# First loads of x and context by batch, and transposes of the identity in TensorE's waits

## What is computed

```
x = x + tanh(g_xattn[l]) * xattn(layernorm(x), ctx)     # 32 query heads, 8 key/value heads of 128
x = x + tanh(g_ffn[l])   * ffn(layernorm(x))
# xattn: q = h @ Wq.T; k, v = ctx @ Wk.T, ctx @ Wv.T; q, k = rmsnorm(q), rmsnorm(k)
#        softmax(q k^T / sqrt(128) + mask) @ v, then @ Wo.T
```

## Time and profile before

| | |
|---|---|
| median of 3 runs | 1437.88 us |
| the profiled execution | 1436.61 us, its span 1434.8 us |
| TensorE (matmul) busy | 1364.0 us, 95% |
| VectorE, ScalarE, GpSimd busy | 959.0, 846.6, 629.4 us |
| mean granted TensorE clock | 0.982 |
| chain that ended last | TensorE 69%, issue 12%, VectorE 8%, GpSimd 6% |

### The profile page before, as it was taken

How to read it: one execution, slowest core, us unless ns; L and a number is a source line. 1 busy time by engine, 2 the same in 40 slices (tenths; PEclk the granted TensorE clock), 3 DMA queues, 4 the chain that set the end, 5 groups by cost and what they waited for, 6 DMA issues and landing times.

```text
span 1434.8 us, 26304 instructions
## 1 busy us (share of the span) xinstructions
PE 1364.0 (95%) x7915; PEld 1143.1 (80%) x7924; DVE 959.0 (67%) x1971; ACT 846.6 (59%) x3270; POOL 629.4 (44%) x667
## 2 busy tenths in 40 slices
PE   5999999999999999987878899999999999999897
PEld 4888888888888888864645688888888888888786
DVE  4678787887878786477777655555555555557565
ACT  4656666666666666655455566566656666665341
POOL 2437666565656575443333334333333334341132
PEclk9899999999999999998989999999999999999999
DMA  7011210211111111001000110101010100100001
GB/s 272 1 51 47 64 51 18 78 36 55 51 62 51 57 51 57 31 1 45 1 29 1 35 48 30 45 29 44 29 44 29 44 29 23 50 0 1 0 16 45
DMA packets 33688, 59.23 MB, mean 41 GB/s; under 512 B 2784, under 2 KB 25952, under 8 KB 29536
## 3 DMA queue, kind: packets, MB, share of 16 engines
q1 hardware_dynamic: 33632, 58.54, 12.3%
HBM read 56.43 MB, written 2.10 MB: 41 GB/s over the span
## 4 chain that ended last, share of the span: by engine, by line
PE 69%; issue 12%; DVE 8%; POOL 6%; ACT 3%; DMA 1%; SPq 0%; POOLq 0%; DVEq 0%; ACTq 0%
PE bank L958 49%; PE bank L950 7%; PE bank L1034 6%; PE bank L1095 5%; POOL w_lo L398 2%; DVE amax L734 1%; DVE f_q L741 1%; POOL rstd L430 1%; DVE f_s L758 1%; POOL ln_rstd L420 1%; PE bank L1086 1%; PE bank L967 1%; DVE f_iq L752 1%; ACT L534 1%; POOL x_sb L498 1%
## 5 line engine op out<-in xcount | busy, mean ns | idle before, releaser
L398 POOL TENSOR_TENSOR w_lo<-w_raw,w_hi (+1 forms) x150 | 232.5, 1563 | 208.4 <-ACT w_hi L550 207.7
L567 ACT ACTIVATE squares<-bank 128x128 bf16<-128x128 f32 x512 | 134.8, 278 | 265.4 <-PE bank L958 265.4
L855 DVE SCALAR_TENSOR_TENSOR probs<-bank,mask_sb 128x512 f32<-128x512 f32 x128 | 88.2, 689 | 228.9 <-PE bank L1034 228.8
L607 ACT ACTIVATE probs<-probs,negmax 128x128 f32<-128x128 f32 x512 | 198.6, 390 | 4.4 <-DVE negmax L859 4.0
L426 POOL TENSOR_TENSOR meansq<-sumsq,scalars 128x5 f32<-128x5 f32 x128 | 27.9, 218 | 324.7 <-ACT squares L567 324.7
L430 POOL TENSOR_TENSOR rstd<-meansq,scalars 128x5 f32<-128x5 f32 x128 | 154.1, 1204 | 10.9 <-POOL meansq L426 1.3
L808 DVE TENSOR_TENSOR oT_lo<-bank,oT_hi 128x512 fp32r<-128x512 f32 x128 | 88.2, 689 | 96.7 <-ACT oT_hi L542 96.6
L958 PE MATMUL bank<-w_hi,oT_hi 128*128 (+1 forms) x512 | 150.1, 415 | 0.0
L958 PE MATMUL bank<-w_hi,xT_hi 128*128 (+1 forms) x512 | 142.6, 401 | 0.6 <-DVE w_lo L682 0.6
L958 PE MATMUL bank<-w_lo,oT_hi 128*128 (+1 forms) x512 | 138.2, 391 | 0.0
L958 PE MATMUL bank<-w_lo,xT_hi 128*128 (+1 forms) x512 | 138.1, 392 | 0.0
(11 more groups left out here) (132 smaller groups left out, 3056.1 us busy)
## 6 DMA issues: line engine op xcount, KB each, us to landing
w_raw<-in_wq SPq DMA_DIRECT2D x16, 1024.0 KB, 4.9
w_raw<-in_wo SPq DMA_DIRECT2D x16, 1024.0 KB, 4.8
fw_raw<-in_ffn_w SPq DMA_DIRECT2D x36, 192.0 KB, 2.3
w_raw<-in_wk SPq DMA_DIRECT2D x16, 256.0 KB, 5.3
w_raw<-in_wv SPq DMA_DIRECT2D x16, 256.0 KB, 5.4
x_sb<-in_x SPq DMA_DIRECT2D x4, 512.0 KB, 9.9
ctx_raw<-in_ctxT SPq DMA_DIRECT2D x4, 512.0 KB, 10.5
out<-x_sb SPq DMA_DIRECT2D x8, 256.0 KB, 2.0
```

Source lines behind the costliest of these rows:

```text
L398: last = nc.gpsimd.tensor_tensor(lo, raw, hi.bitcast(FP32), ALU.subtract)
L567: last = nc.scalar.activation(squares[:, h // 2, (b + 1) % 4, h % 2, :], psQ[:, h * P:(h + 1) * P], ACT.Square, scale=SCALE, accum_out=sum ...
L607: last = nc.scalar.activation(probs[:, h * P:(h + 1) * P], probs[:, h * P:(h + 1) * P], ACT.Exp, bias=negmax[:, h:h + 1], accum_out=rowsum ...
L855: nc.vector.scalar_tensor_tensor(heads(probs[:, :]), heads(psSQ[:, :]), SCALE, mask_sb[:, :].unsqueeze(1).to_broadcast([P, REP, P]), ALU.m ...
```

## The change

x and context are loaded in five transfers each, of batches 0, 1, 2-3, 4-5 and 6-7. The first query weights come in two halves with a semaphore each, ahead of batch 1's x and context and of norms and mask. The context is split one batch at a time, batch b + 1 as the last item of step b, and TensorE waits for batch b ahead of its context product. TensorE transposes the identity into an unused bank: 40 times at its start, 10 times ahead of the first context product, and 12, 8 and 6 times in steps 0, 1 and 2 ahead of the transpose of the key.

```diff
+LOADS = ((0, 1), (1, 2), (2, 4), (4, 6), (6, 8))
+LOAD_OF = [i for i, (b0, b1) in enumerate(LOADS) for _ in range(b0, b1)]
+WARM_START, WARM_FILL = 40, {0: 12, 1: 8, 2: 6}
...
             load_x(0)
             load_kv(0, 0, loaded_kv0)
             load_ctx(0)
+            half = WKV0 // 2
+            for i in range(2):
+                sp.dma_start(w_raw[:, i * half:(i + 1) * half],
+                             wq[0:1].rearrange("g p n -> p (g n)")[:, i * half:(i + 1) * half]).then_inc(loaded_q0[i], 16)
+            load_x(1)
+            load_ctx(1)
             sp.dma_start(norm_sb[:, :], norms).then_inc(loaded_small, 16)
             sp.dma_start(mask_sb[:, :], mask).then_inc(loaded_small, 16)
-            load_q(0, 0, loaded_q0)
-            load_x(1)
-            load_ctx(1)
+            load_x(2)
+            load_ctx(2)
             load_wo(0, 0, loaded_wo0)
-            for t in (2, 3):
+            for t in (3, 4):
...
-            def ctx_upper(t):
-                pair = slice(2 * t * P, (2 * t + 2) * P)
-                act.wait_ge(loaded_ctx[t], 16)
-                nc.scalar.activation(ctx_hi[:, :, pair], ctx_raw[:, :, pair], ACT.Copy).then_inc(ctx_hi_done, 1)
+            def ctx_upper(b):
+                act.wait_ge(loaded_ctx[LOAD_OF[b]], 16)
+                tok = xT_tile(b)
+                nc.scalar.activation(ctx_hi[:, :, tok], ctx_raw[:, :, tok], ACT.Copy).then_inc(ctx_hi_done, 1)
...
-                if kind == FIRST and b in (0, 2, 4):
-                    ctx_upper(b // 2 + 1)
+                if kind == FIRST and b + 1 < BATCHES:
+                    ctx_upper(b + 1)
...
-            act.wait_ge(loaded_q0, 16)
-            first_upper(Q_PIECES)
+            for i in range(2):
+                act.wait_ge(loaded_q0[i], 16)
+                first_upper(Q_PIECES[2 * i:2 * i + 2])
...
-                if kind == FIRST and b in (0, 2, 4):
-                    ctx_lower(b // 2 + 1)
+                if kind == FIRST and b + 1 < BATCHES:
+                    ctx_lower(b + 1)
...
                     if kind == FIRST:
-                        pe.wait_ge(ctx_lo_done, b // 2 + 1)
+                        if b == 0:
+                            keep_clock(10)
+                        pe.wait_ge(ctx_lo_done, b + 1)
...
                 if has(n, 0):
 
+                    if kind == FIRST:
+                        keep_clock(WARM_FILL.get(b, 0))
                     pe.wait_ge(kn_done, n + 1)
...
+            def keep_clock(count):
+                for _ in range(count):
+                    nc.tensor.transpose(psA[:, 0:P], ident[:, :], ident[:, :])
+
             pe.wait_ge(consts, 2)
+            keep_clock(WARM_START)
             pe.wait_ge(ln_xn, 1)
```

More of the change, by code:

```diff
@@ L213, in flamingo_kernel @@
         loaded_small, loaded_gates = sem("loaded_small"), sem("loaded_gates")
-        loaded_x = [sem(f"loaded_x{i}") for i in range(4)]
-        loaded_ctx = [sem(f"loaded_ctx{i}") for i in range(4)]
-        loaded_kv0, loaded_q0, loaded_wo0 = sem("loaded_kv0"), sem("loaded_q0"), sem("loaded_wo0")
+        loaded_x = [sem(f"loaded_x{i}") for i in range(len(LOADS))]
+        loaded_ctx = [sem(f"loaded_ctx{i}") for i in range(len(LOADS))]
+        loaded_kv0, loaded_wo0 = sem("loaded_kv0"), sem("loaded_wo0")
+        loaded_q0 = [sem(f"loaded_q0_{i}") for i in range(2)]
         loaded_qkv, loaded_wo = sem("loaded_qkv"), sem("loaded_wo")
@@ L308, in load_x @@
             def load_x(t):
-                sp.dma_start(x_sb[:, 2 * t:2 * t + 2, :],
-                             x.rearrange("(b p) d -> p b d", p=P)[:, 2 * t:2 * t + 2, :]).then_inc(loaded_x[t], 16)
+                b0, b1 = LOADS[t]
+                sp.dma_start(x_sb[:, b0:b1, :], x.rearrange("(b p) d -> p b d", p=P)[:, b0:b1, :]).then_inc(loaded_x[t], 16)
             def load_ctx(t):
-                pair = slice(2 * t * P, (2 * t + 2) * P)
-                sp.dma_start(ctx_raw[:, :, pair], ctxT[:, :, pair]).then_inc(loaded_ctx[t], 16)
+                tok = slice(LOADS[t][0] * P, LOADS[t][1] * P)
+                sp.dma_start(ctx_raw[:, :, tok], ctxT[:, :, tok]).then_inc(loaded_ctx[t], 16)
             def load_group(before, slot, q=None):
@@ L682, in first_lower, with ctx_lower @@
                 nc.vector.tensor_tensor(lo, raw, hi.bitcast(FP32), ALU.subtract).then_inc(first_lo, 1)
[L684 to L687, removed]
+            def ctx_lower(b):
+                tok = xT_tile(b)
+                dve.wait_ge(ctx_hi_done, b + 1)
+                nc.vector.tensor_tensor(ctx_lo[:, :, tok], ctx_raw[:, :, tok], ctx_hi[:, :, tok].bitcast(FP32),
                                         ALU.subtract).then_inc(ctx_lo_done, 1)
@@ L810, in step @@
                 if kind == FIRST and b + 1 < BATCHES:
-                    if (b + 1) % 2 == 0:
-                        dve.wait_ge(loaded_x[(b + 1) // 2], 16)
+                    dve.wait_ge(loaded_x[LOAD_OF[b + 1]], 16)
                     moments(b + 1, b + 1)
```

## The result

Six runs of each kernel gave medians of 1443.01 us (1440.88 to 1445.17) after the change and 1437.79 us (1434.26 to 1439.07) before it: ratio 1.0041, 95% interval 1.0026 to 1.0056, so the change costs 5.2 us by the medians and 5.9 us by the ratio. The profiled execution took 1442.29 us with a span of 1440.5, 5.7 more than before.

The account below looks back on a forecast made before the run. TensorE, busy 1364.0 of 1434.8 us, was taken as the bound, so early delays reach the end. Front +0.4, waits +10.9, fills 0 and clock 0 gave +11.3 us: forecast 1449 us, range 1438 to 1453.

Parts of the forecast that it names:

- the waits: TensorE waiting for ctx_lo before context products of steps 1 to 7: about 3 us twice, then about 1.2 five times.
- +10.9: Sum over the steps up to step 7's context product: new context waits less late x and key time regained, in us.
- the same 6.4 us on both sides, 0: Steps 1 to 3: low-clock stretches cost 6.4 us before and after the change, so no difference.
- the front: Start to end of first query product: bounds +0.9 and -0.1 us at low clock, -4.8 at high; +0.4 taken.
- The two stretches that I set against it: Old-kernel 34.92 to 38.33 and 45.16 to 48.58 us: taken as evidence that transposes leave the clock low.
- The prediction's own sign for this: First 40 transposes: speeding up to 0.11 us each before 9 us would mean rival 1 or rival 2 holds.
- rival 1: Transposes raise the clock, new waits let it fall again; front -3.9, 1 us saved in steps 1 to 3: 1444; chance 0.27.
- rival 2: TensorE never falls to 1.2 GHz in the first 90 us: -0.3 us, 1437.6, not slower; chance 0.13.
- rival 3: Clock also falls in steps 3 to 6, each border having 1.2 us empty; two falls +3.4 us: 1452.6; chance 0.10.
- the forecast of +11.3: Whole kernel: front +0.4, waits +10.9, fills 0, clock in steps 1 to 3 0; 1449 us; chance 0.50.
- The loads: Front: less queued ahead of the last query half, so the first query product could start at 14.2, not 16.71 us.
- The fills in steps 0 to 2: 12, 8 and 6 transposes before the key's wait fit at high clock, delay by tenths at low; 0 taken.

Follow-up runs that it names:

- e8: The changed kernel with the context still split by single batches but one step earlier, batch 1 ahead of the steps: 1429.48 us, ratio 0.9963.
- e4: The kernel before with only the 76 transposes of the identity added, no other load or split order: 1435.35 us, ratio 0.9995.
- e9: The changed kernel with 27 and 30 more identity transposes ahead of TensorE's context waits in steps 1 and 2: 1441.61 us, ratio 1.0042.
- e5: The changed kernel with context split in pairs a step or more ahead of use, and no identity transposes: 1433.71 us, ratio 0.9983.
- e7: The changed kernel with context in early pairs and only the first 50 identity transposes, none in steps 0 to 2: 1432.48 us, ratio 0.9981.
- e3: The changed kernel with context split in pairs a step or more ahead of use, loads and transposes kept: 1431.56 us, ratio 0.9970.
- e1: The changed kernel with ScalarE's split of the next context ahead of the output pieces in steps 0 and 1: 1439.16 us, ratio 1.0025.

## Why the prediction was right, and where not

**The direction and the waits were right.** The waits came as named: 3.10 and 3.44 us ("about 3 us twice") and 1.38, 1.29, 1.29, 1.29, 1.29 ("about 1.2 us five times"), 13.1 in all. The chain of qT, output pieces, upper and lower half is in the trace: in step 0 the lower half ends 3.00 us behind the start of qT (24.95 - 21.95), where the prediction took 29.5 - 26.48 = 3.02, and e8, which differs from the change in the lead alone, removes the loss.

**The sum behind them, +10.9, agrees with 10.86 by luck, because two errors cancel.** What follows is an estimate from one profiled execution of each kernel. Without low stretches the kernel before takes 90.21 - 21.40 = 68.8 us from the end of the first query product to C(7) (e4, where that product ends at 21.40), and the change 80.46 - 4.18 = 76.3 (with e9's 4.18): the waits are worth 7.5 net, not 10.9. And "the same 6.4 us on both sides, 0" is wrong: the low clock cost 69.60 - 68.8 = 0.8 us before and about 4.2 after, 3.4 net. The likely cause of both is one. In the kernel before, steps 1 to 3 were late for x and the key at either clock (e4), so neither a faster TensorE nor a shorter path was worth its full size there.

**The step that failed is the front.** "I take the low clock and +0.4" measured -4.07. The transposes do bring the clock up. The two stretches that I set against it, 2.99 us busy without a rise and 2.04 with a fall, also had waits in them, the 6.57 us of transposes have none. The sentence of the Trainium skill ("TensorE: Matmul & The Clock Gate", Part 4), that the full clock doesn't engage in transpose mode, does not hold for these float32 transposes: in the changed kernel the clock stood at 2.4 GHz from 6.23 us, when TensorE had done nothing else. The prediction's own sign for this, transposes at 0.11 us before 9 us, is there. The measured time is that of rival 1 (1444), below the forecast's own 1446 to 1452; the whole range holds it because it was drawn from rival 2 to rival 3. These 4.5 us and 1.1 that the span gives back behind C(7) are the distance to the forecast of +11.3. The 1.1 are of the size of the late low stretch above, which is at 1338.8 to 1345.6 us in the kernel before and absent in the change; no run isolates it.

**Rival 1 named the mechanism, but its 1 us saved by the clock in steps 1 to 3 was not there:** the low clock cost more after the change than before it. For the same reason rival 2's -0.3 could not have come: by the estimate above, with both low stretches gone C(7) would be near 98.22 - 4.2 = 94.0, still 2.6 behind the kernel before.

**The loads did what the working says**, 14.74 for 14.2, and they were not idle in the result: e5, with them and early pairs but no transposes, is at 0.9983. No run has the loads alone. The fills in steps 0 to 2 fitted into the wait for the key, as taken: behind them TensorE still waited 1.42, 0.97 and 0.74 us for the key.

**Rival 3** was not seen in the change: with 1.29 us empty at each border the clock held in steps 3 to 6. In e9 it fell at 49.94, in step 3.

## What to carry to other kernels

Making a piece smaller is free only if it keeps its lead: ask for each consumer how many instructions of the producer's list now stand between its last input and the piece, and whether the consumer executes in order. Work that stands last in one engine's step and is wanted first in another's next step is late by its whole chain. A low clock came near to costing half of the busy time only where nothing else of the step was late (4.2 us of 4.8 in e9, 0.9 of 6.4 in e4); run the fill alone first, before counting its gain. Making pieces even does not shorten their sum: in steps 4 to 6 it moved time from the long steps to the short ones.

## What the runs showed of the hardware

- While 40 transposes of a float32 identity ran back to back from 2.00 us on, the full clock came at 6.23 us; in e9, e7, e8, e4, e3 and e1 the first rise was at 5.57, 6.42, 6.59, 6.74, 8.17 and 8.26. Without them it came at 13.55, 19.34, 19.59, 20.97 and 21.27.
- With transposes in the waits of about 3 us the clock stayed at 2.4 GHz from 19.22 to 49.94 us (e9); with TensorE idle in them it fell at 23.30 and 36.95 (the change).
- Where VectorE and GpSimd subtract at the same time, either can pay. In the change VectorE's split of 128x512 took 0.82 us beside GpSimd's pieces and 0.69 where GpSimd did nothing, and GpSimd's two took 2.95. In the kernel before GpSimd's two took 2.54 and VectorE's split of 128x1024 took 2.19 instead of 1.22.
